# Where the fill of the expert slots is issued in ScalarE's instruction stream

## The reference, cut to what matters

```
x = x + layernorm(attention(layernorm(x)))          # rotary, causal, 512 keys
h = x' + latent_attention(rmsnorm(x'))              # rotary on half of each head, causal
out = h + shared_expert(rmsnorm(h)) + sum over the best 2 of 7 routed experts
x = x + layernorm(out)
```

## Time and profile before

| | |
|---|---|
| median of 3 runs | 2561.5 us (2555.55 to 2562.26) |
| the profiled execution, its time | 2555.55 us |
| its span, first to last instruction | 2553.8 us |
| mean granted TensorE clock | 0.94 of full speed |
| PE busy | 86% |
| DVE, ACT, POOL busy | 61%, 41%, 39% |
| DMA packets, mean rate | 386 MB, 151 GB/s |

### The profile page before, as it was taken

One profiled execution on the slowest core, in us unless ns is written; L12 is line 12 of the kernel. 1 busy time (PEld: TensorE's weight loads), 2 busy tenths in 40 slices (PEclk: granted clock), 3 DMA queues, 4 the chain that ended last, 5 costly groups with the idle time before them and its releaser, 6 DMA issues. The chain is left out here.

```text
span 2553.8 us, 38025 instructions
## 1 busy us (share of the span) xinstructions
PE 2198.5 (86%) x12992; PEld 1511.8 (59%) x12992; DVE 1548.6 (61%) x4168; ACT 1042.2 (41%) x2164; POOL 990.9 (39%) x1049
## 2 busy tenths in 40 slices
PE   6898899989889999898898988984998999999600
PEld 4665565666645656565565655642776788888500
DVE  3656766656567565666666666654564655655377
ACT  1435453334544333455433454542331455555300
POOL 1545634446464534555354455450433000000174
PEclk9999999999999999999999998986999999999855
DMA  5434554544535534354543443434455555555497
GB/s 172 113 110 125 146 161 116 141 117 116 142 110 159 155 108 116 100 150 143 155 130 102 114 128 100 108 83 141 167 203 203 194 183 211 191 200 204 155 325 251
DMA packets 228430, 386.11 MB, mean 151 GB/s; under 512 B 24718, under 2 KB 108558, under 8 KB 222606
## 3 DMA queue, kind: packets, MB, share of 16 engines
q1 hardware_dynamic: 157710, 290.87, 38.4%
q10 hardware_dynamic: 60288, 59.25, 6.8%
q0 software_dynamic: 10240, 33.56, 3.5%
HBM read 141.90 MB, written 140.51 MB: 111 GB/s over the span
## 5 line engine op out<-in xcount | busy, mean ns | idle before, releaser
L638 ACT ACTIVATE probs<-scoresT 128x512 f32<-128x512 f32 (+3 forms) x1024 | 417.3, 436 | 543.7 <-PE scoresT L1023 538.5
L819 DVE CUSTOM_DVE_ANT_0 unused<-score,mask 128x128 bf16<-128x128 f32 (+3 forms) x1024 | 465.6, 485 | 259.4 <-PE score L1000 245.5
L1000 PE MATMUL score<-stacks 96*128 96x256 f32 (+2 forms) x1024 | 388.0, 422 | 50.0 <-DVE rowmax L819 48.2
L1023 PE MATMUL scoresT<-stacks 97*128 97x256 f32 (+2 forms) x1024 | 404.5, 430 | 20.0 <-ACT probs L638 10.1
L571 POOL TENSOR_TENSOR probs<-probs 128x1536 f32<-128x1536 f32 (+1 forms) x128 | 372.8, 2913 | 45.9 <-PE out_ps L1037 38.0
L1000 PEld LDWEIGHTS score<-stacks 96*128 96x128 f32 x1024 | 180.0, 191 | 249.3 <-issue 178.5
L832 DVE RECIPROCAL total<-total 128x128 f32<-128x128 f32 x256 | 232.7, 932 | 96.5 <-ACT whole L649 91.2
L930 PE MATMUL middle<-wqkv,XT 128*128 128x128 f32 x2048 | 268.1, 278 | 7.0 <-ACT XT L605 6.1
L560 POOL TENSOR_SCALAR_AFFINE_SELECT probs<-probs 128x512 f32<-128x512 f32 x256 | 163.7, 640 | 281.7 <-ACT probs L638 281.5
L930 PEld LDWEIGHTS middle<-wqkv,XT 128*128 128x128 f32 x2048 | 258.4, 193 | 22.0 <-issue 8.4
L1023 PEld LDWEIGHTS scoresT<-stacks 97*128 97x128 f32 x1024 | 186.5, 192 | 123.6 <-ACT probs L638 71.4
(11 more groups left out here) (174 smaller groups left out, 3793.1 us busy)
## 6 DMA issues: line engine op xcount, KB each, us to landing
stacks<-parts SPq DMA_DIRECT2D x768, 128.0 KB, 2.5
x_slots<-mask ACTq DMA_DIRECT2D x56, 1024.0 KB, 4.8
xr<-x_slots SPq DMA_DIRECT2D x22, 1024.0 KB, 6.0
y_slots<-y SPq DMA_DIRECT2D x22, 1024.0 KB, 4.3
raw<-in_gates SPq DMA_DIRECT2D x23, 512.0 KB, 3.9
raw<-in_ups SPq DMA_DIRECT2D x23, 512.0 KB, 4.9
raw<-in_downs SPq DMA_DIRECT2D x23, 512.0 KB, 5.7
normed<-in_L_attn_x SPq DMA_DIRECT2D x8, 1024.0 KB, 8.6
```

Of the source, the lines that this page charges most:

```text
L638: act.activation(probs[j][:, h, 0:width], scoresT[:, u % ST_BANKS, first:first + width], ACT.Exp, scale=SCALE).then_inc(exp_done, 1)
L819: ins = dve.tensor_tensor_reduce(unused[:, t, 0:width], score.bank(name)[:, first:first + width], mask[:, T - width:T], 1.0, MASKED, ALU.a ...
L1000: ins = pe.matmul(score.bank(name)[:, first:first + width], heads[0:ROWMAX, 0, h, t * P:(t + 1) * P], heads[0:ROWMAX, 1, h, 0:width], star ...
L1023: pe.matmul(scoresT[:, u % ST_BANKS, 0:T - first], heads[0:ROWMAX + 1, 1, h, j * P:(j + 1) * P], heads[0:ROWMAX + 1, 0, h, first:T], start ...
```

## The change

ACT's issue of `clear(k)` moves. It stood behind the exponentials that precede the step ("PV", k, 1), at share 0.55 of group k. It now stands in the branch of the step ("O", k), directly behind the two copies of `take_output(k)`, at the start of group k+1. The number of fills, their size and their data are the same.

```diff
                     if step == "O":
                         take_output(*which)
-                    if step == "PV" and which[1] == 1 and which[0] < NR * blocks:
-                        clear(which[0])
+                        if which[0] < NR * blocks:
+                            clear(*which)
                     if step == "ST":
                         exps(*which)
```

## The result

| | before | after |
|---|---|---|
| median of 6 runs | 2558.0 us (2554.0 to 2562.3) | 2619.8 us (2616.7 to 2626.2) |
| the profiled execution's span | 2553.8 us | 2622.0 us |
| mean granted TensorE clock | 0.94 | 0.932 |

The ratio is 1.0245, with a 95% interval of 1.0226 to 1.0264. I had forecast 2572 us, with a range of 2553 to 2588, so the result lies 32 us above it. As a difference I had 10.9 us, and 61.8 were measured.

A forecast was written before the change was run, and what follows sets the result against it. PE was taken to bound the kernel, paying for late stacks pieces: stalls 18.6 us, less 3 that DVE gives back, less 4.7 for the removed gap, made +10.9 us on the 2561.5 median, so 2572 us, range 2553 to 2588.

The forecast's parts named there:

- What bounds the kernel, and the lead: PE pays stalls at products of stacks; time from first piece's issue to first use is 3.7 us at six boundaries.
- The old place is worth nothing: Middle of the group: a group takes 28.1 us with or without its fill, so leaving ordinarily gains nothing.
- ACT's issue at no cost: Group boundary: the 0.59 us issue lies in ACT's idle time before the exponentials; uncovered, up to 0.6 us.
- The maxima stay in front, and the jam goes: Row maxima land before the fill; the gap behind 1 MB loads disappears, gaining 2.95 + 1.7 = 4.7 us.
- The delay of the third piece: Last stacks piece of the first head at a boundary: 1.8 us later, bounds 0.6 and 2.6 us.
- the wait added from the store: SP's h_kept store behind a fill, read as 1.1 us added wait for a piece of stacks.
- shared turns: Third piece alternating with the fill's packets after its wait: 64 / 16 x 47 ns = 0.2 us.
- The 0.5 us for the first piece: Third piece: some 0.5 us added because the first piece uses engines during the fill; a piece is 0.64 us of work.
- The upper bound: Third piece's delay at most 2.6 us, from two pieces issued into a full jam that took 5.0 us.
- the jam that moves to the boundary: Rival: pieces lose 2.6 us or more, six to nine clock falls add 1.7 us each; about 2600 us, chance 0.09.
- The alternation by packets: Rival: queues merely alternate, pieces lose 0.6 us at most, stalls 4.0 us at most; 2561 us, chance 0.26.
- the order of issue decides: Boundary DMAs: a shared descriptor generator, locked during one DMA, makes issue order decide; stalls sum to 18.6 us.

The follow-up runs named there:

- pv2: Changed kernel with the fill on ACT's queue issued at step PV(k, 2), one step later than the old place; 2559.6 us, ratio 0.9991.
- sp_behind: Changed kernel with the fill issued by SP on its own queue behind all 12 pieces of stacks, none by ACT; 2563.5 us, ratio 1.0022.
- o_eighth: Changed kernel with only 1/8 of each fill at the boundary, the rest at the old place; 2559.6 us, ratio 0.9998.
- o_quarters: Changed kernel with the whole fill at the boundary as four DMAs of 256 KB on ACT's queue; 2690.3 us, ratio 1.0502.
- o_half: Changed kernel with 1/2 of each fill at the boundary, the other half at the old place; 2570.4 us, ratio 1.0039.
- o_halffine: As the kernel with 1/2 of each fill at the boundary, but in packets of 512 B; 2570.9 us, ratio 1.0045.
- o_pair: Changed kernel with the fill as two DMAs of 512 KB, issued back to back by ACT at the boundary; 2628.3 us, ratio 1.0284.
- o_wide: Changed kernel with the same 1 MB fill read from a weight tile in packets of 8 KB; 2587.7 us, ratio 1.0117.
- o_dram: Changed kernel with the fill's source in device memory, its packets 64 KB in the trace; 2614.6 us, ratio 1.0221.
- pool_wait: Changed kernel with the fill on GpSimd's queue at the same moment, after waiting for the sums, packets of 4 KB; 2635.9 us, ratio 1.0282.
- pool_pair: Changed kernel with the fill on GpSimd's queue at the same moment as two transfers of 512 KB; 2637.3 us, ratio 1.0328.

## Why the prediction was wrong

**What bounds the kernel, and the lead: right.** PE pays what it waits for at line 1000. With the leads read before, a third piece late by 3.9 us gives stalls of 76.2 us at 41 boundaries; the weight loads of the changed kernel waited 74.1 us, 38 times. The products, whose waits are what the kernel pays, stood for 61.7 us, 34 times, so the leads give somewhat too much. One reading behind them was not what I called it: at n = 16 and 34 the third piece landed late already, 5.1 and 5.0 us after the first issue, and my 5.1 and 4.0 us are 3.7 plus the spare time after its landing. From first issue to first use are 6.5 and 5.3 us there. For the sum the spare time is the right number.

**The old place is worth nothing: right.** Kernels that move the fill away from it and disturb nothing (pv2, sp_behind) gain nothing that can be told.

**ACT's issue at no cost: right**, by the row at 259.36 with 0.48 us of idle time, and by o_eighth. o_quarters shows where the cover ends.

**The maxima stay in front, and the jam goes: right**, but worth less. PE's wait for `negmax` fell by 2.5 us, not by 2.95, and the 1.7 us of clock that I added are lost among the new falls.

**The delay of the third piece: the step that failed.** I wrote that the fill "makes a later transfer wait until a part of its 1024 packets is gone, and then takes a turn for each turn of the other", and took 1.8 us, 2.6 at most. Measured are 3.9 us. The form was right and the sizes were not, in two ways. First, I took the wait added from the store in the earlier trace rows, whose first packet came 1.1 us late. A store of 1 MB shares for long, and its landing of 7.1 us would have been the better sign; for a piece, which is a few packets on each engine, what counts is when its last packet gets through. Second, I charged 0.2 us for shared turns. The runs show in its place that the third piece is complete only when the whole fill is through. At n = 8 some 646 of its 1024 packets went before the second piece moved one, not the 431 of the prediction, and the other third was not passed either. 1 MB at the 47 ns a packet of the prediction is 1024 / 16 x 47 ns = 3.0 us of all engines, which is the greater part of the 3.9. That the delay follows the bytes (o_eighth, o_half, o_halffine, the whole) and the order of issue (o_pair, o_quarters) bears this out. The 0.5 us for the first piece rested on a wrong reading too: 0.64 us is the time from issue to issue, not the engines' work of a piece. The upper bound came from two pieces issued late into a jam, when much of the fill was through already, so it was no upper bound.

The sum follows: the same leads give 18.6 us at 1.8 and 76.2 at 3.9. The stall is steep in the delay, since only 6 boundaries have a lead of 3.7 us but 41 one below 7.6. Of these 76, DVE gave back 48.2 - 32.9 = 15.3 us, where I had 3 for the small stall.

**The clock: left out of the sum.** PE's gaps of up to 3.8 us were followed by stretches at 0.50, 13 more than before in the profiled executions, for some 9 to 22 us of PE's busy time. I had priced such falls in one rival alone, at six to nine. That rival, the jam that moves to the boundary, had the right kind and sign and 0.09 of the chance. It gave 2600; its sum too went by 2.6 us for the pieces, where 3.9 were measured.

**Turns and order.** The alternation by packets that the Trainium skill states in DMA: Bandwidth & Descriptors, Queues, rings and completion order, does not describe 260.2 to 261.8 us, in which 560 packets of q10 and none of q1 were moved, 35 for each engine; here the measurement decides. It agrees better with the stretch behind, in which both queues moved packets. That the order of issue decides, which I had drawn from the shared descriptor generator that the Trainium skill describes in Perfetto Trace Analysis, DMA Instruction — HWDGE (DVE, Sync), agrees with o_pair and o_quarters. But GpSimd's fills, in the runs with its queue, did the same harm, so the generator is not shown to be the cause.

**What stays open.** Whether the pieces' packets stand ready in the engines and are passed over, or are written only when the fill's are through. No record in these traces shows the moment at which a descriptor is written. Also open is why o_wide with 3.2 us costs 29 us and o_dram with 3.5 costs 54. PE's products waited 33.5 and 50.8 us for stacks, and the second head is later in the latter (9.1 us after the first issue, against 8.4), but I did not test whether that is all of it.

## What to carry to other kernels

A large transfer that nobody waits for is not free: it costs what it puts in front of small transfers that somebody does wait for. Here that was about the engines' time for all of its bytes, on each of the three queues tried. Before one is moved, read for each small transfer behind it how long it has from its issue to its first use, add the whole engine time of the large one, and sum what exceeds the lead; if gaps in TensorE's work of some microseconds come out, add the clock that is lost after them. If it must be issued there, place it behind the last small transfer, or well ahead of the first.

## What the runs showed of the hardware

- Two hardware queues shared the engines only late: after a fill of 1 MB was issued on q10, a piece of 128 KB issued 0.5 us later on q1 moved its first packet behind some two thirds of the fill (n = 8) and landed after 5.8 us (median) instead of 2.4, and the queue of the issuing engine made little difference (late by 3.1, 3.9 and 4.3 us on SP's, ACT's and GpSimd's).
- SP's issues are held in turn: an instruction of line 428 usually takes 0.60 us, and 2.04 us at this boundary while the fill was under way. The fifth and sixth pieces are therefore issued late as well. With GpSimd's fill (pool_wait) SP's issues at n = 8 last up to 2.06 us too, so this is no sign of something that SP and ACT alone share.
- GpSimd's queue moved the same fill in packets of 4 KB that ACT's queue moved in packets of 1 KB: q0 has 25472 packets in pool_wait and 10240 in the changed kernel, which is 272 for each fill, where q10 has 1024. Two DMAs of alternate stretches of 1 KB (pool_pair) had 288, so those were packets of 4 KB as well. ACT's queue had packets of 1, 8 and 64 KB for the fill in the changed kernel, o_wide and o_dram.
- After PE had stood for 3.80 us the granted clock was 1.00 in the next stage of work (265.6 to 266.4 us) and then 0.50 for over 3 us.
